# Long attention in pairs of bodies: scores of both ahead of the transposes of both, and a closer drain for the last two chunks

## What is computed

```python
q = (x @ wq).reshape(B, T, KV, REP, 128); k, v = latent projections, one per KV group
scores = einsum('bqhrd,bkhd->bhrqk', q, k) * scale        # causal mask, T = 1024
y = einsum('bhrqk,bkhd->bqhrd', softmax(scores), v);  long = y @ wo
for i in range(6):
    x = attn_layer(shift_tokens(x), ...) + x              # windows of 32, 16 heads of 64
    x = ffn_layer(shift_tokens(x), ...) + x               # LN, W1, a * gelu(gate), W2
```

## Time and profile before

| | us |
|---|---|
| median of 3 runs (1980.29 to 1985.61) | 1985.2 |
| profiled execution | 1979.53 |
| its span, first to last instruction | 1977.7 |
| PE busy | 1821.4 (92%) |
| DVE / ACT / POOL busy | 1506.0 / 1326.3 / 1395.9 |
| one iteration of the long attention | 80.0 |

### The profile page before, as it was taken

How to read it: one execution, slowest core, us unless ns; L and a number is a source line. 1 busy time by engine, 2 the same in 40 slices (tenths; PEclk the granted TensorE clock), 3 DMA queues, 4 the chain that set the end, 5 groups by cost and what they waited for, 6 DMA issues and landing times.

```text
span 1977.7 us, 70559 instructions
## 1 busy us (share of the span) xinstructions
PE 1821.4 (92%) x29444; PEld 1294.7 (65%) x29444; DVE 1506.0 (76%) x2292; ACT 1326.3 (67%) x2149; POOL 1395.9 (71%) x1492
## 2 busy tenths in 40 slices
PE   6888778789999999999999999999999999999995
PEld 5666656456667666666666666666766666667664
DVE  5866867678887878787877877788787778887872
ACT  4666777466677667667766776667667766776664
POOL 3323323888888778788778877788877888877761
PEclk9999999999999999999999999999999999999997
DMA  4000000000001000010000000000100000000000
GB/s 173 2 0 0 0 1 2 1 5 9 3 7 43 3 2 14 3 47 3 3 14 2 24 26 3 13 2 3 48 2 2 14 2 2 3 3 2 8 8 12
DMA packets 12453, 25.44 MB, mean 13 GB/s; under 512 B 1856, under 2 KB 9728, under 8 KB 10496
## 3 DMA queue, kind: packets, MB, share of 16 engines
q1 hardware_dynamic: 12160, 21.18, 3.2%
HBM read 20.13 MB, written 1.05 MB: 11 GB/s over the span
## 4 chain that ended last, share of the span: by engine, by line
PE 63%; ACT 8%; issue 6%; DVE 3%; POOL 1%; ACTq 0%; DVEq 0%; POOLq 0%
PE banks L1137 23%; PE banks L1398 14%; PE banks L1339 10%; PE banks L1422 7%; PE banks L1384 5%; PE banks L1373 2%; ACT L810 2%; ACT arena L706 2%; DVE arena L1002 1%; ACT arena L810 1%; ACT L813 1%; DVE small L1031 1%; ACT arena L717 1%; PE banks L1444 1%; DVE prob L1055 1%
## 5 line engine op out<-in xcount | busy, mean ns | idle before, releaser
L1398 PE MATMUL banks<-M,xs 128*32 128x512 f32 x3072 | 367.7, 595 | 0.3 <-DVE prob L1055 0.2
L474 POOL TENSOR_TENSOR arena<-arena 128x1024 f32<-128x1024 f32 x96 | 229.7, 2392 | 157.3 <-DVE arena L1002 157.3
L746 ACT ACTIVATE arena<-banks 128x1024 f32<-128x1024 f32 x192 | 197.3, 1028 | 118.5 <-PE banks L1398 117.2
L1049 DVE TENSOR_REDUCE small<-banks 128x16 f32<-128x1024 f32 x96 | 117.5, 1224 | 204.3 <-PE banks L1384 204.3
L997 DVE TENSOR_TENSOR arena<-banks,tabs 128x1024 f32<-128x1024 f32 x192 | 233.4, 1215 | 37.3 <-ACT arena L706 33.5
L1002 DVE TENSOR_TENSOR arena<-banks,tabs 128x1024 f32<-128x1024 f32 x192 | 232.9, 1213 | 0.0
L479 POOL TENSOR_TENSOR arena<-arena 128x1024 f32<-128x1024 f32 x96 | 229.0, 2385 | 0.0
L1422 PE MATMUL banks<-arena 128*32 128x128 f32 x6144 | 188.9, 275 | 13.8 <-DVE arena L1088 13.4
L1339 PE MATMUL banks<-cst,arena 128*128 128x128 f32 x1536 | 200.2, 273 | 0.1
L1339 PEld LDWEIGHTS banks<-cst,arena 128*128 128x128 f32 x1536 | 176.7, 140 | 23.3 <-issue 2.6
L469 POOL TENSOR_TENSOR prob<-prob,small 128x1024 f32<-128x1024 f32 x96 | 184.0, 1917 | 10.4 <-DVE small L1039 10.4
(11 more groups left out here) (129 smaller groups left out, 4153.2 us busy)
## 6 DMA issues: line engine op xcount, KB each, us to landing
arena<-in_wvo_dram SPq DMA_DIRECT2D x6, 1024.0 KB, 4.9
qkraw<-in_wqk_dram SPq DMA_DIRECT2D x6, 1024.0 KB, 4.7
W<-in_w_dram SPq DMA_DIRECT2D x6, 341.0 KB, 3.0
W<-in_w_dram SPq DMA_DIRECT2D x6, 192.0 KB, 2.4
res<-in_x_dram SPq DMA_DIRECT2D x4, 256.0 KB, 3.7
tabc<-in_tab_dram SPq DMA_DIRECT2D x1, 1024.0 KB, 9.6
out_dram<-res SPq DMA_DIRECT2D x4, 256.0 KB, 3.0
sca_s<-in_sca_dram SPq DMA_DIRECT2D x6, 128.0 KB, 4.9
```

The lines of the kernel that those rows point to most:

```text
L474: pool.tensor_tensor(kc, kc, ks, ALU.add).then_inc(s["k_add"], 1)
L746: act.activation(vw[:, (2 * k + g) % RV, :], two(V_BANK), ACT.Copy).then_inc(s[f"v_cp{g}"], 1)
L1398: ins = pe.matmul(bk(V_BANK + z)[WIN * q:WIN * (q + 1), :], xs[:, b, t0:t0 + WIN], M[:, q, :, :].rearrange("p m n -> p (m n)"), start=True ...
```

## The change

On PE the long attention is issued by pairs: scores L_(p+2), scores s_(p+1), transposes L_p, then `project` if one is due, transposes s_p, then `outputs`. On DVE: scale L_p, inverse and scale of s_p, then cap and peak of L_(p+2) with `add_out` behind it, cap and peak of s_(p+1), inverse of L_(p+1). On ACT the order of copies and exps stays; `copy_outputs` goes behind the exp. In the drain `chunk_at` puts chunks 22 and 23 one G earlier, the gelu table is loaded after the last `roots`, and the last chunk's gelus no longer reload the ln/exp table.

```diff
         def chunk_at(G, lag):
-            c = (G - lag) // 4
-            return c if (G - lag) % 4 == 0 and 0 <= c < DEPTH * NC else None
+            last = 4 * (DEPTH * NC - 2)
+            g = G - lag if G - lag < last - 1 else G - lag + 1
+            return g // 4 if g % 4 == 0 and 0 <= g // 4 < DEPTH * NC else None
...
                     evacuate(j)
+                    if ahead(j) is not None:
+                        exps(ahead(j))
                     for i in due(j, 1, 2):
                         copy_outputs(i)
-                    if ahead(j) is not None:
-                        exps(ahead(j))
...
+                    if k == LAST_TILE + 4:
+                        act.preload_act_table_set("gelu_and_others")
...
-                    if j in LAST_GELUS:
+                    if j in LAST_GELUS and c < DEPTH * NC - 1:
                         act.preload_act_table_set("natural_log_exp_and_others")
...
-                for j in range(len(bodies)):
+                for j in range(0, len(bodies), 2):
                     normalise(j)
+                    inverse(j + 1)
+                    normalise(j + 1)
                     if ahead(j) is not None:
                         cap(ahead(j))
-                    if j < LAST:
-                        inverse(j + 1)
-                    if ahead(j) is not None:
                         peak(ahead(j))
                     for i in due(j, 2, 3):
                         add_out(it, i)
+                    if ahead(j + 1) is not None:
+                        cap(ahead(j + 1))
+                        peak(ahead(j + 1))
+                    if j + 1 < LAST:
+                        inverse(j + 2)
...
-                for j in range(len(bodies)):
-                    if ahead(j) is not None:
-                        scores(ahead(j))
+                for j in range(0, len(bodies), 2):
+                    for e in (j, j + 1):
+                        if ahead(e) is not None:
+                            scores(ahead(e))
                     if more and j == LAST - 1:
                         queries(it + 1, range(3))
-                    if more and j == LAST:
+                    finish(j)
+                    for i in due(j, 2, 3):
+                        project(i)
+                    if more and j == LAST - 1:
                         queries(it + 1, range(3, 6))
-                    for i in due(j, 1, 2):
-                        outputs(i)
-                    finish(j)
-                    if not more and j == LAST - 2:
+                    finish(j + 1)
+                    if not more and j == LAST - 3:
...
-                    for i in due(j, 2, 3):
-                        project(i)
+                    for i in due(j + 1, 1, 2):
+                        outputs(i)
```

## The result

| | median us | runs | ratio to before, 95% interval |
|---|---|---|---|
| before | 1980.3 (1976.8 to 1985.6) | 7 | |
| changed | 1993.9 (1989.3 to 1996.3) | 7 | 1.0065 [1.0049, 1.0081] |

The change makes the kernel slower, by 0.65% or 13 us of 1980. The prediction said slower, 1991 us between 1974 and 2002, and 6 us more than before: the sign and the mechanism are right, the size is half of what was measured. That 1991 lies so near to 1993.9 is luck in part: the forecast was put on the median of three runs, 1985.2 us, and seven runs have 1980.3. The profiled execution of the changed kernel has a span of 1992.1 us against 1977.7.

What follows compares the result with a forecast made beforehand. A ring of waits through DVE's short scale and PE's short transposes was taken to set the long attention's pace. Four iterations at +2.5 us (+10) and the drain at -4 gave +6 on 1985.2: 1991 us, range 1974 to 2002.

Steps and rivals of the forecast that it cites:

- The ring through the short transposes: Long attention before: DVE peak, short scale, PE short transposes, long scores, DVE cap; 3.70 us a pair, opened by the change.
- Ring A: New first-group loop of DVE and ACT through the short exp's sum, long peak to long peak: 3.93 us against 3.70.
- The sum of the way from the scale of L0 to the cap of L15: Each long-attention iteration: 53.6 for 13 steps, 1.1 start, 2.7 outputs; 57.4 us against 54.2, 3.2 more.
- What comes back behind the cap of L15: Each iteration's end: 0.7 us regained, bounds 0 and 1.2; last short scores and transposes no longer wait behind outputs.
- ring B: New loop of ACT and PE through short exp, short scores, long transposes and long exp: 4.3 us in the last group.
- The drain: Kernel's end: -1.4 gate 0, -1.3 and -2.6 table loads, +0.7 gate 1, +0.5 late tile 95; taken as -4 us.
- gate 1: Drain: with the table loads gone, gelu 1 starts only when gate 1 is there, costing back about 0.7 us.
- The move of the chunks: Drain: tile 95 starts about 3 us later, net +0.5; gate 0 of chunk 23 waits less, -1.4 us.
- The exp on the ring: Faster rival's deciding point: short exp with sum must end within 1.66 us of the long peak; rows have 1.91.
- the case of DVE's own pace: Faster rival in the long attention: short exp off the ring, pairs at 3.6 us, total 1967 us; chance 0.24.
- The clock case: Rival: PE falls to half its clock in the last group, 3 us more an iteration, 2003 us; chance 0.07.
- Cancelling: Rival for the whole kernel: gains and losses cancel within 0.3%, or 6 us, say 1985 us; chance 0.29.

Runs made afterwards that it cites:

- e10: Changed kernel plus one unused ACT copy of 256 columns behind each long exp from L2 on, delaying the short exp; ratio to before 1.0113.
- e11: Kernel before plus the same unused ACT copy behind each long exp from L2 on; ratio to before 1.0010.
- e7: Changed kernel with POOL's split of the next queries also waiting for the cap that follows the scores; ratio to before 1.0061.
- e6: Changed kernel with the short body ahead of the long in each pair for scores, cap, peak, copy and exp; ratio to before 1.0229.
- e8: Kernel before with the drain's gelu table edits alone, chunks 22 and 23 at their old places; ratio to before 0.9963.

## Why the prediction was right in sign and short in size

*What bounds the kernel.* Right. The ring through the short transposes is there before and gone after, and PE's wait for DVE ahead of them with it.

*Rings A and B.* Right, and shown by e10 against e11: only in the new order does a later short exp cost time in the first three iterations (2.0 us each, against nothing). Ring A's 3.93 us were measured to the hundredth once the split is out of the way (e7).

*The sum of the way from the scale of L0 to the cap of L15*, predicted 57.4 us, measured 58.4. By its terms: the start 1.06 us (1.1 predicted); two first-group steps 4.15 each (3.93), 0.44 more, which is the collision of the scale with the split; the next four steps, with the first outputs, 17.3 (17.3); the four after them 17.5 (17.6); the last three 14.25 (13.5), 0.75 more, which is the copy that waits 0.71 us for `outputs`. That wait is named in the lines of `evacuate`, and in the traces of the changed kernel and e6; no run takes it away alone, so its price is argued from the rows. By the kernel before, the way has grown by 0.4 us at the start, 0.6 in the first two steps, 0.1 in the next four, 1.2 in the four after them and 1.9 in the last three: most of the loss is in its last seven steps, where the short bodies are longer.

*What comes back behind the cap of L15*, predicted 0.7 us, is the term that failed: nothing came back. From there to the next iteration it is 19.4 us against 19.3 in the third. PE waits there 1.81 us for the last short exp, ring B once more, where it waited 0.91 and 0.93 us for DVE before:

```profile
270.75 0.49 PE L1144 MATMUL banks<-xnw,gqs 128*128 x1 [1.81 <-ACT arena L645]
```

```profile
257.55 0.65 PE L1279 MATMUL banks<-cst,arena 128*128 128x128 f32 x4 [0.91 <-DVE arena L930]
...
259.13 1.14 PE L1279 MATMUL banks<-cst,prob 128*128 128x128 f32 x5 [0.93 <-DVE prob L930]
```

The cap of s15 does come 0.8 us earlier behind that of L15 (4.75 us against 5.59 at the full granted clock), but only because its scores now stand ahead of the transposes of L14; these have to be done behind it, and from the cap of s15 to the next iteration's first cap it is 16.4 us and not 15.4, again at the full clock. Without the 0.7 and with the two missed terms the third iteration loses 4.4 us, not 2.5. The first three lose 3.0, 5.5 and 4.4, together 12.9; their spread is that of the clock behind the cap of L15, not of the rings.

*The fourth iteration*, +2.6 us against +2.5 counted, agrees by luck: the way grew by 3.5 us (55.7 to 59.2), and 0.9 came back behind it, where the clock scatters.

*The drain*, predicted -4, measured -3.1 in this pair of profiled executions and -4.0 by the means above. The total hides two errors that offset each other. The table edits give more than the 3.2 us counted, 5.7 by the means: gate 1 didn't cost back 0.7, and the last down-projection, no term of the sum, took 2.9 us in each of the eight executions with the table edits and 4.4 in the mean of the six without them (2.9 to 5.5). Why it ran at the higher clock stays open. The move of the chunks seems to cost some 1.7 us where -1.4 and +0.5 were counted: tile 95 starts 4.6 us later and not 3, and 3.0 of it come back. The rule weighed there, a drain on top of each table load (the Trainium skill, page "ScalarE: Activation LUTs", section "What ACT_TABLE_LOAD costs"), fails here as well: in the changed kernel the gelu behind the load of 1958.52 starts 1.30 us after it.

*The rivals.* The exp on the ring decided as the rows had it: DVE waits for the short exp, so the case of DVE's own pace didn't come. The clock case didn't either: from the scale of L0 to the cap of L15 the granted clock is 1.00 in all four iterations, before and after. Cancelling failed because the rings are longer, not shorter, than walked.

*The whole*: +15.5 - 3.1, and +2.8 of scatter in the layers and -0.7 ahead of the first iteration, are the 14.4 us to rounding between the two spans; by the medians it is 13, of which 6 were predicted.

## What to carry to other kernels

When an order is changed to take an engine's wait out of a ring, write down for every instruction that moved what now wants the last result of each other engine at once: the new ring is found there, and ring A, summed from old rows, came out right to the hundredth. Then go through all waits of the instructions beside the moved one, those too that were always met: `outputs` behind the transposes made a copy wait that no trace of before could show. And look at which engines work at the same time, and on what memory, in the new order; a duration from the old trace holds only beside its old neighbours.

A loss that sits in an interaction isn't found by undoing halves: here each half cost as much as the whole or more. To delay the suspected result by a known amount, in both orders, told more than any undoing.

## What the runs showed of the hardware

A DVE scale between two places of SBUF and a POOL TENSOR_TENSOR slow each other: 0.28 to 0.50 us for the one of 128 columns, 0.40 to 0.95 us for the other beside a scale of 1024 columns (216.46 to 217.41; the scale ran from 216.40 to 217.15). Beside DVE's cap and peak, which read PSUM, POOL's split keeps its 0.40 us (in the pair of the earlier trace rows from 205.52, beside the cap of 205.48 and the peak behind it). The Trainium skill states this, page "SBUF — State Buffer", section "Who interferes with whom": DVE and GpSimd share a pair of ports, and when a tensor_scalar runs in a two-port mode, whichever of the two engines issues first has the pair for its whole instruction and the other is blocked until then. The trace agrees: the split that began 0.06 us behind the long scale ended 0.26 us behind its end, and the short scale that began at 213.38, 0.04 us behind the split's second instruction, ended 0.08 us behind the end of that. Read beside the new order, the rule would have pointed at the 0.22 us a step that the prediction left out.

The TensorE clock makes executions of the same instructions differ. The last down-projection took 4.94 us before, where PE had waited 2.23 and 2.06 us ahead of it, and 2.92 in e8, where it had waited 0.95 and 0.25 (granted clock 0.69 and 0.91 in that stretch). It looks as if idle time of PE is paid for a second time, but e11 had waits of 2.23 and 1.67 us in the same drain, and 2.92 us. In the long attention, too, the step from the cap of L15 to that of s15 took 5.59 us at a granted clock of 1.00 in the second iteration of before and 6.55 at 0.83 in the third. A gain of 1 or 2 us that shows in one execution is held against others of the same code before it is put down to an edit.
